# The FFN's last 64 inner rows: two tiles at a time on the two halves of the array's rows, each tile in a PSUM bank of its own

## The chip, the core and the metric

The kernel runs on one core of one Trainium2 chip, in one launch. A core has five engines with an instruction stream each: TensorE (PE; its weight loads are shown apart as PEld), VectorE (DVE), ScalarE (ACT), GpSimd (POOL) and SyncE (SP), which issues most of the DMA transfers. They meet at semaphores. Matmuls write to PSUM, which has 8 banks of 512 f32 in each of 128 partitions. The metric is the device time of one execution in microseconds (us).

## The reference, cut to what matters

Two layers work on x, 4 x 256 rows of 256 numbers (1,024 tokens, 8 tiles of 128 rows): a graph attention and an FFN, then a sparse graph step and a mixture of experts with two experts chosen per token. The change concerns the FFN of the first layer:

```python
g = jnp.einsum('th,ih->ti', xf, gate_w) * gate_s      # gate_w: 704 x 256
u = jnp.einsum('th,ih->ti', xf, up_w) * up_s          # up_w:   704 x 256
hdn = jax.nn.silu(g) * u
out = jnp.einsum('ti,hi->th', hdn, down_w) * down_s   # down_w: 256 x 704
```

Its result is added to x by way of a gate. The inner size 704 is five times 128 and 64 more. All of it is in f32.

## The kernel before, in words

The FFN works on two halves `h` of four tiles each. `ffn_up(h, it)` makes chunk `it` of the inner rows for the half's 512 tokens: PE multiplies the gate's weights (`gw`) and the up weights (`uw`) with the turned input `xnT`, ACT takes the silu into `th`, and DVE multiplies that with the up product into `hT` (L1475). Chunk 5 holds the last 64 inner rows: the 64 gate columns and the 64 up columns stand side by side in `gw`, so one product has the gate in rows 0 to 63 and the up product in rows 64 to 127; ACT writes rows 64 to 127 of `th`, DVE rows 64 to 127 of `hT`, and rows 0 to 63 of `hT` and of the down weights `dw` are zero.

`ffn_down(p, i)` (L2027) sums the six chunks for tile `i` of pair `p` in half a bank (banks 4 and 5), and DVE adds a pair's result to x (L1484). Every f32 matmul stands in the trace as two records, each with a weight load of its own; so a tile of `ffn_down` has twelve records and the FFN's two products with chunk 5 are two times four.

Nothing is scheduled automatically. `PE_ORDER`, `ACT_ORDER`, `DVE_ORDER` and `POOL_ORDER` are lists written by hand, and each engine walks through its list in order. So what stands behind a waiting step waits too. Around the change these steps stand in the lists:

- `lost` (L2039), `keep` (L1223, L1229) and `kept` (L2052): the sparse graph's exact threshold. DVE searches in small pieces (`search`, L1147 to L1177), PE counts the rows that the search has lost, DVE reads that flag and makes `a2`, PE turns `a2` in banks 6 and 7.
- `router` (L2072), `choices` to `ranks`, `count` (L2085), `list` (L2104) and `ids` (L1698, L1699): the experts' scores, and from them the list of the tokens of each expert. With `ids(0)` POOL gathers the tokens' rows (L699), and PE turns them in `turn_x` (L2114).
- `up1`, `up3` (both L2128) and `down` (L2160): the experts. `down(0)` waits until DVE has made the third pair's x (`attn_out`, L1513).
- SP loads `dw` and the scales `dsr` in `load_down` (L550 to L553), and DVE multiplies them in `scale_down` (L1271, L1272).

Of the kernel before, what the change touches and what calls it, by code (L numbers as in the profile page):

```python
# [63 lines left out]
def build(nc, x_in, ctx2_in, g_xattn, g_ffn, gamma, w0_in, w0T_in, b0_in, w1_in, w1T_in, a_in, b1_in,  # L64
# [5 lines left out]
    with ctx:  # L70
# [2262 lines left out]
```

## Time and profile before

| | us |
|---|---|
| median of 2 runs | 215.81 (215.25 to 216.37) |
| the profiled execution, as a run | 216.97 |
| its span in the trace | 215.1 |

The span is read from the first to the last instruction; the execution's own time has 1.9 us around it. Records of PE are pipelined: the ends are modelled, and how fast a stream goes is read from start to start. A group of records in the timeline has the start of the first, the time to the end of the last, and behind "x" how many there are. The granted clock is at its full level from 0 to 203 us of the span, and at 0.72 of it on the mean over the last 12 us.

### The profile page before, as it was taken

The numbers are of one execution on the slowest core, as the hardware profiler recorded it, in microseconds if no ns is written. First come the engines' busy times: TensorE is split into PE (matmuls) and PEld (weight loads), VectorE is DVE, ScalarE is ACT, GpSimd is POOL, SyncE is SP. The second block draws the span as 40 slices with busy tenths as digits, with TensorE's granted clock in tenths as the row PEclk, the third lists the DMA queues.
The fourth block names the chain that finished last, engine by engine and source line by source line (L and its number), as shares of the span: only waits on it lengthen the run. The fifth ranks groups of instructions, "written<-read, shape, count | busy, mean of one in ns | idle before, by whom it ended". The sixth has DMA issues, their size and how long they took to land.

```text
span 215.1 us, 3843 instructions
## 1 busy us (share of the span) xinstructions
PE 201.7 (94%) x1286; PEld 159.0 (74%) x1286; DVE 136.5 (63%) x469; ACT 84.9 (39%) x187; POOL 84.7 (39%) x107
## 2 busy tenths in 40 slices
PE   8999979999999999989999999999999999999930
PEld 7787854435786447869899999999963599999920
DVE  3497897999997989997987796933318511211210
ACT  2678662998300457033434272222226322222100
POOL 8175326620001120045460334667768155434143
PEclk9999999999999999999999999999999999999985
DMA  6838409219999216817044222232423210122224
GB/s 183 214 157 254 130 26 274 59 38 382 411 420 417 91 49 213 318 38 247 30 123 145 29 24 24 47 46 49 80 57 42 55 10 4 13 24 24 25 23 45
DMA packets 16795, 26.06 MB, mean 121 GB/s; under 512 B 4105, under 2 KB 12421, under 8 KB 16774
## 3 DMA queue, kind: packets, MB, share of 16 engines
q1 hardware_dynamic: 11328, 20.14, 26.0%
q0 software_dynamic: 4064, 5.24, 13.9%
q10 hardware_dynamic: 1382, 0.41, 1.1%
q8 instruction: 11, 0.18, 0.4%
q14 instruction: 10, 0.08, 0.1%
HBM read 21.34 MB, written 5.51 MB: 125 GB/s over the span
## 4 chain that ended last, share of the span: by engine, by line
PE 48%; DVE 22%; DMA 13%; issue 7%; POOL 3%; ACT 2%; POOLq 2%; DVEq 1%; ACTq 0%
PE PS L2128 13%; PE PS L2160 8%; DMA out_dram<-a,ids_late 8%; PE PS L2013 4%; DMA out_dram<-zb,sidx 4%; PE PS L1831 4%; PE PS L2180 3%; PE PS L2027 3%; PE PS L1895 2%; PE PS L2193 2%; DVE hT L1475 2%; ACT a L854 2%; PE PS L2072 2%; DVE x L1335 2%; DVE a L1229 1%
## 5 line engine op out<-in xcount | busy, mean ns | idle before, releaser
L2128 PE MATMUL PS<-hT,e 128*128 128x128 f32 x512 | 61.7, 275 | 0.0
L2128 PEld LDWEIGHTS PS<-hT,e 128*128 128x128 f32 x512 | 60.0, 192 | 1.0 <-issue 0.4
L2013 PE MATMUL PS<-xnT,e 128*128 128x512 f32 x88 | 39.5, 597 | 1.2 <-ACT xnT L923 0.8
L2013 PEld LDWEIGHTS PS<-xnT,e 128*128 128x128 f32 x88 | 16.2, 190 | 21.2 <-issue 17.4
L1731 DVE TENSOR_TENSOR hT<-th,PS 128x512 f32<-128x512 f32 x15 | 10.3, 687 | 32.5 <-PE PS L2128 31.1
L2160 PE MATMUL PS<-e,hT 128*128 128x256 f32 x128 | 30.4, 381 | 0.2 <-DVE x L1513 0.2
L2160 PEld LDWEIGHTS PS<-e,hT 128*128 128x128 f32 x128 | 23.2, 190 | 2.9 <-issue 0.3
L656 POOL TENSOR_TENSOR rstd<-veps,nhalf 128x2 f32<-128x2 f32 x12 | 8.7, 727 | 39.3 <-DVE veps L1092 39.2
L722 POOL DMA_INDIRECT out_dram<-a,ids_early x8 | 13.2, 1646 | 22.4 <-ACT a L1017 8.5
L2027 PE MATMUL PS<-e,hT 128*128 128x256 f32 x96 | 21.9, 383 | 0.0
L993 ACT ACTIVATE th<-PS 128x512 f32<-128x512 f32 x16 | 9.5, 593 | 26.7 <-PE PS L2128 26.7
L2027 PEld LDWEIGHTS PS<-e,hT 128*128 128x128 f32 x96 | 17.8, 190 | 2.8 <-issue 0.5
L722 POOL DMA_INDIRECT out_dram<-a,ids_late x7 | 11.1, 1581 | 15.1 <-DMA out_dram<-a,ids_late 10.8
L699 POOL DMA_INDIRECT sim<-xn_rows,ids_early x8 | 8.4, 1055 | 19.0 <-DVE ids_early L1699 13.8
L678 POOL DMA_INDIRECT e<-graph_rows,gix x8 | 9.2, 1156 | 9.7 <-DMA graph_rows<-e 8.0
L951 ACT ACTIVATE x<-x,rs 128x256 f32<-128x256 f32 x8 | 4.4, 594 | 19.4 <-DVEq L1507 19.4
L1831 PE MATMUL PS<-ones 128*128 128x128 f32 x64 | 10.8, 326 | 1.0 <-POOL ones L608 1.0
L1831 PEld LDWEIGHTS PS<-ones 128*128 128x128 f32 x64 | 9.5, 230 | 1.6 <-POOL ones L608 1.0
L1017 ACT ACTIVATE a<-PS,coef_early 128x256 f32<-128x256 f32 x8 | 3.8, 473 | 15.8 <-PE PS L2160 15.8
L854 ACT ACTIVATE a<-sim,bar 128x256 f32<-128x256 f32 x16 | 7.9, 497 | 3.8 <-DVE bar L1122 3.8
L699 POOL DMA_INDIRECT sim<-xn_rows,ids_late x8 | 8.4, 1046 | 2.4 <-issue 2.1
L1475 DVE SCALAR_TENSOR_TENSOR hT<-th,us,PS 128x512 f32<-128x512 f32 (+1 forms) x12 | 8.9, 746 | 0.2
(314 smaller groups left out, 321.3 us busy)
## 6 DMA issues: line engine op xcount, KB each, us to landing
e<-e_in SPq DMA_DIRECT2D x24, 512.0 KB, 8.3
x<-x_in SPq DMA_DIRECT2D x2, 512.0 KB, 5.9
graph_rows<-e SPq DMA_DIRECT2D x4, 256.0 KB, 2.2
out_dram<-x SPq DMA_DIRECT2D x4, 256.0 KB, 2.7
xn_rows<-xn SPq DMA_DIRECT2D x4, 256.0 KB, 2.6
e<-gw_in SPq DMA_DIRECT2D x1, 768.0 KB
e<-uw_in SPq DMA_DIRECT2D x1, 640.0 KB
e<-dw_in SPq DMA_DIRECT2D x1, 640.0 KB, 4.4
```

The lines of the kernel that those rows point to most:

```text
L678: pool.indirect_dma_start(out=picked[:, t, :], out_offset=None, in_=f_dram[b], in_offset=bass.IndirectOffsetOnAxis(ap=gix[:, t:t + 1], axi ...
L699: pool.indirect_dma_start(out=xg[j % E], out_offset=None, in_=xn3_dram[0:(HN, B * N)[h], :], in_offset=bass.IndirectOffsetOnAxis(ap=ids[h] ...
L722: pool.indirect_dma_start(out=out, out_offset=bass.IndirectOffsetOnAxis(ap=row_of, axis=0), in_=yv[kept_in(j)], in_offset=None, bounds_che ...
L854: ins = act.activation(a2[:, t, :], sim[:, t, :], ACT.Sign, bias=bar[:, n, t:t + 1], accum_out=signs[:, t:t + 1])
L993: act.activation(th[:, j % 2, :], PS[:, j % 2, :], ACT.Silu).then_inc(silu_ready, 1)
L1475: dve.scalar_tensor_tensor(out=hT[at:P, it, :], in0=th[at:P, n % 2, :], scalar=us[at:P, it:it + 1], in1=PS[at:P, bank, :], op0=ALU.mult, o ...
L1731: dve.tensor_tensor(hh[me], th[:, me, :], PS[:, 2 + me, :], ALU.mult).then_inc(gated, 1)
L1831: pe.matmul(PS[:, bank, 0:P], ones[:, :], ones[:, :], start=True, stop=True)
L2013: mm = pe.matmul(PS[:, bank, :], w[:, k, it * P:(it + 1) * P], xnT[:, h, k, :], start=(k == 0), stop=(k == 1))
L2027: mm = pe.matmul(PS[:, 4 + a // 2, (a % 2) * 256:(a % 2 + 1) * 256], hT[:, it, a * P:(a + 1) * P], dw[:, it, :], start=(it == 0), stop=(it ...
L2128: mm = pe.matmul(PS[:, bank + q, f * P:(f + 1) * P], w[:, k * F + f * P:k * F + (f + 1) * P], xgT[x_at][:, k, :], start=(k == 0), stop=(k ...
L2160: mm = pe.matmul(PS[:, y_bank(j), q * C:(q + 1) * C], hh[q][:, f * P:(f + 1) * P], W2[expert_of(j)][:, f * C:(f + 1) * C], start=(f == 0), ...
```

## The change

The 64 last inner rows of a tile now lie on either half of the partitions: for tiles 0 and 2 of a half of the tokens on rows 64 to 127, for tiles 1 and 3 on rows 0 to 63. `dw` holds the last 64 rows twice, `gw` has 64 columns more (up, gate, up), and the two zero fills on POOL are gone. In `ffn_up(h, 5)` PE multiplies tiles 0 and 2 with one choice of columns and tiles 1 and 3 with another (four matmuls of 2 x 128 columns in place of two of 512), and ACT and DVE do their step in two instructions of 64 x 256 in place of one of 64 x 512. A new step `ffn_tails(p)` multiplies the 64 rows of a pair's two tiles, one on each half of the rows, ahead of the pair's `ffn_down`, which has five chunks left. Each tile sums in a bank of its own (4 to 7 in place of halves of 4 and 5). `lost` moves from bank 6 to bank 3, so `ffn_up(1, 1)` waits until the flag has been read; `kept` waits until the half's sums have been read out of banks 6 and 7.

```diff
+GATE = FULL * P + 3 * TAIL
...
-        gw = e1[:, 5 * 1024:5 * 1024 + 2 * IT * P].rearrange("p (k n) -> p k n", k=2)
+        gw = e1[:, 5 * 1024:5 * 1024 + 2 * GATE].rearrange("p (k n) -> p k n", k=2)
...
+        DOWN_BANK = 4
+        LOST_BANK = 3
...
-                    ("router", 0), ("router", 1), ("ffn_down", 2, 0), ("count", 0), ("ffn_down", 2, 1), ("ffn_down", 3, 0, 0, 3),
-                    ("list", 0), ("ffn_down", 3, 0, 3), ("ffn_down", 3, 1, 0, 4), ("turn_x", 0), ("ffn_down", 3, 1, 4), ("lost", 1),
+                    ("router", 0), ("router", 1), ("ffn_tails", 2), ("ffn_down", 2, 0), ("count", 0), ("ffn_down", 2, 1), ("ffn_tails", 3), ("ffn_down", 3, 0, 0, 4),
+                    ("list", 0), ("ffn_down", 3, 0, 4), ("ffn_down", 3, 1, 0, 4), ("turn_x", 0), ("ffn_down", 3, 1, 4), ("lost", 1),
...
+        LOW, HIGH = slice(0, TAIL), slice(P - TAIL, P)
+        TAIL_ROWS = ((HIGH, LOW), (LOW, HIGH))
+
+        def every_second(ap, i):
+
+            return ap.rearrange("p (a i n) -> p a i n", i=2, n=P)[:, :, i, :]
...
-                sp.dma_start(dw[P - TAIL:P, FULL, :], dw_in[FULL * P:INTER, :]).then_inc(down_loaded, 16)
+                for r in (0, P - TAIL):
+                    sp.dma_start(dw[r:r + TAIL, FULL, :], dw_in[FULL * P:INTER, :]).then_inc(down_loaded, 16)
...
-            pool.memset(dw[0:P - TAIL, FULL, :], 0.0).then_inc(consts, 1)
-            pool.memset(hT[0:P - TAIL, FULL, :], 0.0).then_inc(consts, 1)
...
-                M, to = (P, 0) if it < FULL else (TAIL, P - TAIL)
-                act.activation(th[to:to + M, n % 2, :], PS[0:M, n % 2, :], ACT.Silu,
-                               scale=gs[0:M, it:it + 1]).then_inc(ffn_silu, 1)
+                if it < FULL:
+                    ins = act.activation(th[:, n % 2, :], PS[:, n % 2, :], ACT.Silu, scale=gs[:, it:it + 1])
+                else:
+                    for i, (rows_of_h, rows_of_gate) in enumerate(TAIL_ROWS):
+                        ins = act.activation(every_second(th[rows_of_h, n % 2, :], i), every_second(PS[rows_of_gate, n % 2, :], i),
+                                             ACT.Silu, scale=gs[rows_of_gate, it:it + 1])
+                ins.then_inc(ffn_silu, 1)
...
+                    for i, (rows_of_h, _) in enumerate(TAIL_ROWS):
+                        ins = dve.scalar_tensor_tensor(out=every_second(hT[rows_of_h, it, :], i), in0=every_second(th[rows_of_h, n % 2, :], i),
+                                                       scalar=us[rows_of_h, it:it + 1], in1=every_second(PS[rows_of_h, n % 2, :], i),
+                                                       op0=ALU.mult, op1=ALU.mult)
+                ins.then_inc(ffn_h_ready, 1)
...
-                dve.tensor_tensor(xp, xp, PS[:, bank, :].rearrange("p (t c) -> p t c", t=2),
-                                  ALU.add).then_inc(down_read, 1)
+                dve.tensor_tensor(xp, xp, PS[:, bank:bank + n, 0:C], ALU.add).then_inc(down_read, 1)
...
+                if it == FULL:
+                    for i, first in enumerate((FULL * P + TAIL, FULL * P)):
+                        for k in range(2):
+                            mm = pe.matmul(every_second(PS[:, n % 2, :], i), gw[:, k, first:first + P], every_second(xnT[:, h, k, :], i),
+                                           start=(k == 0), stop=(k == 1))
+                    mm.then_inc(ffn_g_done, 1)
+                    return
+                if h == 1 and 2 + n % 2 == LOST_BANK:
+                    pe.wait_ge(lost_ready, 1)
...
-            def ffn_down(p, i, first=0, stop=IT):
+            def ffn_tails(p):
+
+                first = PARTS[p][0] % HT
+                pe.wait_ge(ffn_h_ready, IT * (p // 2 + 1))
...
+                for i, (rows_of_h, _) in enumerate(TAIL_ROWS):
+                    a = first + i
+                    pe.matmul(PS[:, DOWN_BANK + a, 0:C], hT[rows_of_h, FULL, a * P:(a + 1) * P],
+                              dw[rows_of_h, FULL, :], start=True, stop=False)
+
+            def ffn_down(p, i, first=0, stop=FULL):
+
+                a = PARTS[p][0] % HT + i
                 for it in range(first, stop):
-                    mm = pe.matmul(PS[:, 4 + a // 2, (a % 2) * 256:(a % 2 + 1) * 256],
-                                   hT[:, it, a * P:(a + 1) * P], dw[:, it, :],
-                                   start=(it == 0), stop=(it == IT - 1))
+                    mm = pe.matmul(PS[:, DOWN_BANK + a, 0:C], hT[:, it, a * P:(a + 1) * P], dw[:, it, :],
+                                   start=False, stop=(it == FULL - 1))
...
                 pe.wait_ge(a2_ready, HT * (h + 1))
+                pe.wait_ge(down_read, 2 * (h + 1))
```

Two places in the built programs are needed below. In these rows "e" is the memory of the experts' weights, in which `gw`, `uw` and `dw` lie before the experts come; the lists count matmuls, of which each has two records in the trace.

PE in the second half of the FFN, from the last chunk's product to the step behind `turn_x(0)`. Before:

```order
L2013 MATMUL PS<-xnT,e 128x512 x2
L2072 MATMUL PS<-rg,xnT 128x8 x8
L2027 MATMUL PS<-e,hT 128x256 x6
L2085 MATMUL PS<-Os,before 128x40
L2085 MATMUL PS<-Os,ones 128x40 x4
L2027 MATMUL PS<-e,hT 128x256 x9
L2104 MATMUL PS<-RA,h0T 128x16 x8
L2027 MATMUL PS<-e,hT 128x256 x7
L2114 MATMUL PS<-ident,sim 128x128 x2
L2027 MATMUL PS<-e,hT 128x256 x2
```

In the change (L2031 is the last chunk of `ffn_up`, L2056 `ffn_tails`, L2063 `ffn_down`, L2140 `list`, L2150 `turn_x`):

```order
L2031 MATMUL PS<-xnT,e 128x2x128 x4
L2108 MATMUL PS<-rg,xnT 128x8 x8
L2056 MATMUL PS<-e,hT 128x256 x2
L2063 MATMUL PS<-e,hT 128x256 x5
L2121 MATMUL PS<-Os,before 128x40
L2121 MATMUL PS<-Os,ones 128x40 x4
L2063 MATMUL PS<-e,hT 128x256 x5
L2056 MATMUL PS<-e,hT 128x256 x2
L2063 MATMUL PS<-e,hT 128x256 x4
L2140 MATMUL PS<-RA,h0T 128x16 x8
L2063 MATMUL PS<-e,hT 128x256 x5
L2150 MATMUL PS<-ident,sim 128x128 x2
```

Ahead of `list(0)` stood 6 + 9 = 15 full matmuls; now there are 5 + 5 + 4 = 14 full ones and two pairs on halves. Behind it, up to `turn_x(0)`, stand 5 in place of 7.

DVE at the last chunk of the second half (the DVE list keeps its order). Before:

```order
L1166 MAX top<-work 128x8 x2
L1475 SCALAR_TENSOR_TENSOR hT<-th,us,PS 64x512
L1533 COPY sc<-PS 128x16
L1537 MAX mx<-sc 128x8 x2
L1540 MAX_INDEX ix<-mx,sc 128x8 x2
```

In the change:

```order
L1179 MAX top<-work 128x8 x2
L1492 SCALAR_TENSOR_TENSOR hT<-th,us,PS 64x2x128 x2
L1550 COPY sc<-PS 128x16
L1554 MAX mx<-sc 128x8 x2
L1557 MAX_INDEX ix<-mx,sc 128x8 x2
```

One instruction has become two of half the width, ahead of the reading of the scores; ACT has the same in its `ffn_up` of the last chunk.

## Rows read from the trace of the kernel before

**Rows 1.** The page's first part: busy us, share of the span, instructions.

```profile
PE 201.7 (94%) x1286; PEld 159.0 (74%) x1286; DVE 136.5 (63%) x469; ACT 84.9 (39%) x187; POOL 84.7 (39%) x107
```

**Rows 2.** The chain of waits in order of time, 72 to 110 us: start, us, what.

```profile
73.13 0.76 DVE hT L1475
73.94 7.13 PE PS L2013 x16
...
85.44 2.73 PE PS L2027 x12
...
88.30 3.97 PE PS L2027 x18
92.27 0.20 PE PS L2104 x8
92.49 0.18 DVE rest_early L1698
...
107.14 1.97 PE PS L2160 x8
```

**Rows 3.** PE's timeline at two earlier steps on half rows (64*64, 64*128): start, us.

```profile
19.65 0.38 PE L1895 MATMUL PS<-w1x,h0T 128*128 128x256 f32 x1
19.96 1.07 PE L1847 MATMUL PS<-ctx,wbuf 64*64 64x512 f32 x4
20.97 0.39 PE L1980 MATMUL PS<-norms,ones 128*128 128x5 f32 x2
...
23.16 0.38 PE L1895 MATMUL PS<-w1x,h0T 128*128 128x256 f32 x1
23.47 2.00 PE L1856 MATMUL PS<-ctx,th 64*128 64x256 f32 x16
25.40 0.29 PE L1903 MATMUL PS<-ident,e 128*128 128x128 bf16 x2
```

**Rows 4.** PE's timeline, 40 to 112 us.

```profile
50.26 5.32 PE L2013 MATMUL PS<-xnT,e 128*128 128x512 f32 x12
55.41 7.93 PE L2027 MATMUL PS<-e,hT 128*128 128x256 f32 x36
63.18 0.17 PE L2039 MATMUL PS<-lost,ones 128*128 128x1 bf16 x1
...
69.32 1.04 PE L2052 MATMUL PS<-ident,a 128*128 128x128 f32 x8
```

**Rows 5.** ACT's timeline: four instructions of 256 columns in a row; the last silu.

```profile
7.20 1.57 ACT L883 ACTIVATE zb<-PS,b 128x256 f32<-128x256 f32 x4 [3.69 <-PE PS L1882]
...
83.79 0.68 ACT L944 ACTIVATE th<-PS,gs 64x512 f32<-64x512 f32 x1 [0.94 <-PE PS L2013]
```

**Rows 6.** DVE's timeline, 38 to 85 us.

```profile
38.66 0.35 DVE L1271 TENSOR_SCALAR dsr<-dsr,tg 128x256 f32<-128x256 f32 x1
...
45.71 0.88 DVE L1335 SCALAR_TENSOR_TENSOR x<-e,tg,x 128x256 f32<-128x256 f32 x2
...
52.99 0.75 DVE L1475 SCALAR_TENSOR_TENSOR hT<-th,us,PS 64x512 f32<-64x512 f32 x1
...
68.38 0.68 DVE L1484 TENSOR_TENSOR x<-x,PS 128x512 f32<-128x512 f32 x1
...
71.88 1.22 DVE L1495 TENSOR_TENSOR zb<-a,PS 128x1024 f32<-128x1024 f32 x1
...
84.50 0.75 DVE L1475 SCALAR_TENSOR_TENSOR hT<-th,us,PS 64x512 f32<-64x512 f32 x1
```

**Rows 7.** Who waited for whom: us in total, times, longest us.

```profile
PE PS L2114 <- DMA sim<-xn_rows,ids_early: 1.0, 1, 1.0
...
DVE rest_early L1698 <- PE PS L2104: 0.2, 1, 0.2
```

**Rows 8.** SP's timeline: the issue of the load of the down scales.

```profile
33.64 0.58 SPq L553 DMA_DIRECT2D dsr<-ds_in  x1
```

**Rows 9.** DMA issues: KB each, median us from issue to landing.

```profile
dsr<-ds_in SPq DMA_DIRECT2D x1, 128.0 KB, 4.5
```

More of the change, by code:

```diff
@@ L428, in build @@
                     ("ffn_up", 0, 4), ("turn_ffn", 2), ("turn_ffn", 3), ("ffn_up", 0, 5), ("ffn_up", 1, 0),
-                    ("ffn_down", 0, 0), ("ffn_down", 0, 1), ("ffn_down", 1, 0), ("lost", 0), ("ffn_down", 1, 1), ("ffn_up", 1, 1),
+                    ("ffn_tails", 0), ("ffn_down", 0, 0), ("ffn_down", 0, 1), ("ffn_tails", 1), ("ffn_down", 1, 0), ("lost", 0), ("ffn_down", 1, 1), ("ffn_up", 1, 1),
                     ("kept", 0), ("ffn_up", 1, 2), ("ffn_up", 1, 3), ("ffn_up", 1, 4), ("turn_moe", 0), ("turn_moe", 1), ("ffn_up", 1, 5),
-                    ("router", 0), ("router", 1), ("ffn_down", 2, 0), ("count", 0), ("ffn_down", 2, 1), ("ffn_down", 3, 0, 0, 3),
-                    ("list", 0), ("ffn_down", 3, 0, 3), ("ffn_down", 3, 1, 0, 4), ("turn_x", 0), ("ffn_down", 3, 1, 4), ("lost", 1),
+                    ("router", 0), ("router", 1), ("ffn_tails", 2), ("ffn_down", 2, 0), ("count", 0), ("ffn_down", 2, 1), ("ffn_tails", 3), ("ffn_down", 3, 0, 0, 4),
+                    ("list", 0), ("ffn_down", 3, 0, 4), ("ffn_down", 3, 1, 0, 4), ("turn_x", 0), ("ffn_down", 3, 1, 4), ("lost", 1),
                     ("up1", 0), ("turn_x", 1), ("up3", 0),
@@ L1222, in keep @@
                 dve.wait_ge(lost_counted, h + 1)
-                dve.tensor_scalar(flag[:, 1 + h:2 + h], PS[:, 6, 0:1], 1.0, None, ALU.min).then_inc(lost_ready, 1)
+                dve.tensor_scalar(flag[:, 1 + h:2 + h], PS[:, LOST_BANK, 0:1], 1.0, None, ALU.min).then_inc(lost_ready, 1)
                 dve.wait_ge(lost_ready, h + 1)
@@ L2010, in ffn_up @@
                     pe.wait_ge(xnT_copied, XT["turn_ffn", 2 * h + 1] + 1)
-                for w, bank, ready in ((gw, n % 2, ffn_g_done), (uw, 2 + n % 2, ffn_u_done))[0:2 if it < FULL else 1]:
+                if it == FULL:
[7 more added lines that the diff above has]
+                    pe.wait_ge(lost_ready, 1)
+                for w, bank, ready in ((gw, n % 2, ffn_g_done), (uw, 2 + n % 2, ffn_u_done)):
                     for k in range(2):
@@ L2038, in lost @@
                 pe.wait_ge(found_ready, h + 1)
-                pe.matmul(PS[:, 6, 0:1], ones16[:, :], lost16[:, h:h + 1], start=True, stop=True)\
+                pe.matmul(PS[:, LOST_BANK, 0:1], ones16[:, :], lost16[:, h:h + 1], start=True, stop=True)\
                   .then_inc(lost_counted, 1)
@@ L2199, in _ @@
                          hot=graph_hot, choice=choice, compose=compose, stay_warm=stay_warm,
-                         flag=graph_flag, graph_check=graph_check, turn_ffn=turn_ffn, ffn_up=ffn_up, ffn_down=ffn_down, lost=lost, kept=kept,
+                         flag=graph_flag, graph_check=graph_check, turn_ffn=turn_ffn, ffn_up=ffn_up, ffn_tails=ffn_tails, ffn_down=ffn_down, lost=lost, kept=kept,
                          turn_moe=turn_moe, router=router)
@@ L2287, with columns @@
     full = FULL * P
-    def columns(v, at):
-        last = np.zeros(P, v.dtype)
-        last[at:at + TAIL] = v[full:]
-        return np.concatenate([v[:full], last]).reshape(IT, P).T
+    def columns(v):
+        return np.concatenate([v, v[full:]]).reshape(IT, P).T
     def by_head(layer):
@@ L2317 @@
         "a_in": np.stack([by_head("0"), by_head("1")]), "b1_in": i["L0_xattn_b1"],
-        "gw_in": np.concatenate([i["L0_ffn_gate_w"], i["L0_ffn_up_w"][full:]]).T,
+        "gw_in": np.concatenate([i["L0_ffn_gate_w"][:full], i["L0_ffn_up_w"][full:], i["L0_ffn_gate_w"][full:],
+                                 i["L0_ffn_up_w"][full:]]).T,
         "uw_in": i["L0_ffn_up_w"][:full].T, "dw_in": i["L0_ffn_down_w"].T,
-        "gs_in": columns(i["L0_ffn_gate_s"], 0), "us_in": columns(i["L0_ffn_up_s"], P - TAIL), "ds_in": i["L0_ffn_down_s"],
+        "gs_in": columns(i["L0_ffn_gate_s"]), "us_in": columns(i["L0_ffn_up_s"]), "ds_in": i["L0_ffn_down_s"],
         "wq_in": np.concatenate([i["L1_xattn_Wq"]] * 2, axis=1), "wk_in": i["L1_xattn_Wk"], "rg_in": i["L1_ffn_gate_w"].T,
```

24 lines of the change are left out of this document (12 added, 12 removed).

## The prediction

> **What bounds the kernel now.** The page's first part shows PE busy for 94% of the span and DVE for 63% [rows 1]. That average invites a wrong conclusion, that less work on PE is less time; so I read the chain of waits next, in order of time, around the FFN's sums. From 73.94 to 92.27 us the chain lies on PE without a break: chunks 3 and 4 of the second half, the last chunk, the router, twelve records of `ffn_down`, eighteen more, and the eight of `list(0)`. Then it leaves PE: DVE makes the list's ids at 92.49 and stays on the chain until PE's `down(0)` at 107.14 [rows 2]. The view of who waited for whom has DVE waiting 0.2 us for `list(0)`, and PE waiting 1.0 us for the first gathered rows behind it [rows 7]. So ahead of `list(0)` PE is the bound, and how early `list(0)` stands is what counts; behind it PE has time to spare, and from 107.14 on it is the bound again, with an order that the change leaves alone. What the FFN's first half gains on PE meets a DVE that is behind: `kept(0)` starts at 69.32, `attn(0)` takes its result only at 71.88 [rows 4, 6], and PE's products of 73.94 follow DVE's product of 73.13 [rows 2].
>
> One slot, below, is a full f32 record of 256 columns from start to start: 36 records of `ffn_down` from 55.41 to 63.18, 0.216 us each [rows 4]; one of 512 columns is 5.15 / 12 = 0.43 us.
>
> **What a pair on half rows costs.** The kernel has such steps already [rows 3]. Sixteen half records of 256 columns begin at 23.47 and the next step at 25.40: 1.93 us, where sixteen slots would be 3.45. So two halves do run at once: eight slots are 1.73. But the step pays something beside its slots. From the last full record ahead (23.16) to the first one behind (25.40) it is 2.24 us, and nine slots are 1.94: 0.30 over. The other step is just like one `ffn_tails`, two matmuls on two halves, of 512 columns: from 19.65 to 20.97 it is 1.32 us, and 0.216 + 2 x 0.43 = 1.08: 0.24 over. I take 0.27 for a step that goes from full rows to halves and back. Then the first full record behind it: in the sums of `ffn_down` that begin behind other work, twelve records take 2.73 us in place of 2.59 and eighteen take 3.97 in place of 3.89 [rows 2], 0.08 to 0.14 over; I take 0.11. Together 0.38 for each `ffn_tails`, and what it saves is two slots, 0.43. **One pair at a time gains 0.05 us on PE**, not 0.43, and four of them 0.2 us in the whole kernel, not 1.73.
>
> The Trainium skill, TensorEngine Tiling (Array Packing), section Key Properties, states that a change of the tiling mode drains TensorE; the 0.24 and 0.30 agree with it. The same page's section Theoretical Speedup gives up to 2 times for a small dimension of at most 64, and by that alone four pairs would save 1.73.
>
> **Part by part, on the chain.**
>
> 1. The list stands later. Between the router and `list(0)` stood 12 + 18 = 30 full records. The first two sums have lost a chunk each (four slots less) and `ffn_tails` comes twice (four more), but of pair 3's first tile four chunks stand ahead of the list in place of three: 32 slots. **+0.43 us**, even with switches at no cost.
> 2. The two switches in that stretch. The one of pair 3 lies in the middle of full records: 0.38. That of pair 2 follows the router, whose first full record already pays 0.11, and 0.07 of the way in hides under the wait of part 4: 0.20. **+0.58**; the ends are 0 (all hidden) and 0.9 (0.44 twice).
> 3. The last chunk of the first half. ACT has two silus of 256 columns in place of one of 512: four such instructions in a row take 1.57 [rows 5], so two 0.79, in place of 0.68. DVE has two products in place of one: two of 256 columns take 0.88, one 0.75 [rows 6]. The chain lies on DVE there, and this product at 52.99 is in it, up to PE's 73.94. 0.13 + 0.11, less a few hundredths that ACT is ahead: **+0.2**; ends 0 and 0.3.
> 4. The same in the second half: the silu at 83.79 ends at 84.47 and DVE starts at 84.50 and ends at 85.25, PE's sums follow within 0.2 us. The sums start 0.24 later, less what PE has in hand: **+0.2**; ends 0 and 0.4.
> 5. The product of the last chunk on PE itself: eight records of 256 columns in place of four of 512: 8 x 0.216 = 1.73 and 4 x 0.43 = 1.72. **0**, if the gap between the two runs of 128 columns costs nothing (a rival).
> 6. New waits. `kept(0)` now waits for DVE's second sum, which ends at 68.38 + 0.68 = 69.06, with part 3 at 69.26; it started at 69.32. PE comes there no earlier than before by more than 0.1, and DVE wants its result at 71.88 [rows 4, 6]. `ffn_up(1, 1)` waits for the flag that DVE reads right behind `lost(0)` at 63.18, and PE still has five full matmuls to do. `ffn_tails(3)` waits for the router's scores, read ahead of `count(0)`. **0**; up to 0.3 if DVE is later than I think, and 2.5 us of cover stand behind it.
> 7. The loads. SP issues one transfer more ahead of `dsr`; such an issue takes 0.58, so `dsr`, issued at 33.64 and 4.5 us on its way, lands at 38.7 in place of 38.1 [rows 8, 9], and DVE wants it at 38.66 [rows 6]. **0**; at most 0.2, with 64 KB more in the way. `gw`, 64 KB larger, comes long ahead of the FFN. POOL's two fills stand at the start of the kernel, and no link of the chain comes from them: 0.
> 8. DVE's sums read two banks in place of one, the same 512 numbers: 0; ends -0.1 and +0.1.
>
> Sum: 0.43 + 0.58 + 0.2 + 0.2 = **1.4 us**. The shift passes on: DVE comes to `ids(0)` 1.4 later, works without a wait until `attn_out`, and `down(0)` moves with it. PE's 0.86 us fewer slots behind the list only lengthen its wait for the gathered rows, from 1.0 to about 2. The profiled execution took 216.97 us, so 218.4 for one like it; the median of the two runs is 1.16 lower, 215.81, and from it I forecast **217.2 us**. The ends of the parts give +0.4 to +2.2, so 216.2 to 218.0.
>
> **The rivals.**
>
> - *The switches are hidden* at these places, as weights come ahead of the full matmuls elsewhere. Parts 1, 3 and 4 stay: +0.8, 216.6. Against it: both steps in rows 3 pay. Chance 0.17.
> - *The halves do not overlap here*, say because two matmuls alone give no overlap. Four slots a step in place of two: 2 x 0.43 more on the chain, +2.3, 218.1. Against it: the step of two matmuls at 19.96 did overlap. Chance 0.08.
> - *Not slower: PE's own time decides.* If DVE's chain has slack that the view does not show, the four pairs give 0.2 to 1.7 us: 214.1 to 215.6, say 215.1. For it: 94% busy. Against it: the chain leaves PE twice just where the change acts. Chance 0.13.
> - *Slower by over 2%: the gap costs.* The last chunk's products now read and write two runs of 128 columns with as much between them; no row of before has a matmul of f32 that does so. If such a record took two slots, the eight in each half cost 1.73 more; both halves' lie on the chain (ACT waited 0.94 for PE ahead of the silu at 83.79 [rows 5]): +1.4 + 3.5, 220.7. It decides from 0.18 us more for a record, since 2% are 4.3 us. Chance 0.06. The Trainium skill, PSUM — Partial Sum Buffer, section Specifications (TRN2), states that any non-contiguous access pattern slows matmuls significantly; no run here shows it.
>
> The forecast itself has 0.56.
>
> **The numbers.** Predicted 217.2; for the forecast alone 216.2 to 218.0. The range of 215.3 to 218.7 takes in the hidden switches, halves that don't overlap and half of the not-slower case, with the 0.5 us by which the two runs lie from their median. A measurement of this kernel tells about 2% from no change, 4.3 us; the whole last chunk of the sums is 16 x 0.216 = 3.45 us, so faster by 2% is nearly excluded: 0.02. Slower by 2% has the gap's case and little else: 0.05. Within 2%: 0.93.
>
> **What would show it.** In the profile after: `list(0)` should stand about 1.4 us later than 92.1, with DVE waiting over 1 us for it in place of 0.2; PE's wait for the first gathered rows about 2 us; each `ffn_tails` with four records in two starts, and from the last full record ahead of it to the first behind 0.9 us or more, not 0.65; ACT's and DVE's last chunk 0.1 longer each; and `down(0)` near 108.5. I am wrong if `list(0)` comes at 92.5 or earlier, if `down(0)` moves less than DVE's ids, or if the eight records of the last chunk take over 1.8 us.

## The result, and the profile after

The changed kernel took **219.33 us** (median of 2 runs, 218.97 and 219.70), the kernel before 215.81: ratio 1.0159, 95% interval 1.0103 to 1.0215. Six later runs gave 218.86 (`control` below). The forecast was 217.2, its range ended at 218.7. The profiled execution took 219.70, its span 217.7 (before 216.97 and 215.1).

The page's first part, after; it answers to [rows 1].

```profile
PE 203.3 (93%) x1294; PEld 159.7 (73%) x1294; DVE 136.9 (63%) x471; ACT 85.8 (39%) x189; POOL 84.9 (39%) x105
```

The chain of waits, after (start, us, what), which answers to [rows 2].

```profile
73.74 0.76 DVE hT L1488
74.54 7.13 PE PS L2039 x16
...
92.48 1.92 PE PS L2063 x8
...
95.83 2.91 DMA sim<-xn_rows,ids_early
98.88 0.54 PE PS L2150 x2
```

Before, DVE stayed on the chain from the ids at 92.49 to `down(0)`. Now the chain goes from the gather to PE's `turn_x(0)` (L2150) and stays on PE up to `kept(1)`, ahead of DVE's last steps to `down(0)`: PE itself is late behind its wait.

PE's timeline, after (L2031 last chunk, L2108 router, L2056 `ffn_tails`, L2063 sums, L2121 `count(0)`, L2140 `list(0)`, L2164 `up1(0)`, L2196 `down(0)`).

```profile
82.48 1.89 PE L2031 MATMUL PS<-xnT,e 128*128 128x256 f32 x8
84.21 1.85 PE L2108 MATMUL PS<-rg,xnT 128*128 128x8 f32 x16
86.42 0.70 PE L2056 MATMUL PS<-e,hT 64*128 64x256 f32 x4 [0.36 <-DVE hT L1492]
87.05 2.42 PE L2063 MATMUL PS<-e,hT 128*128 128x256 f32 x10
89.31 0.19 PE L2121 MATMUL PS<-Os,before 128*128 128x40 bf16 x1
...
89.44 2.40 PE L2063 MATMUL PS<-e,hT 128*128 128x256 f32 x10
91.78 0.70 PE L2056 MATMUL PS<-e,hT 64*128 64x256 f32 x4
92.41 1.99 PE L2063 MATMUL PS<-e,hT 128*128 128x256 f32 x8
94.24 0.35 PE L2140 MATMUL PS<-RA,h0T 128*128 128x16 bf16 x8
...
98.88 0.54 PE L2150 MATMUL PS<-ident,sim 128*128 128x128 f32 x2 [2.03 <-DMA sim<-xn_rows,ids_early]
...
100.14 3.12 PE L2164 MATMUL PS<-hT,e 128*128 128x128 f32 x16
...
110.12 1.97 PE L2196 MATMUL PS<-e,hT 128*128 128x256 f32 x8 [0.19 <-DVE x L1530]
```

The same places before (L2027 sums, L2104 `list(0)`, L2114 `turn_x(0)`, L2128 `up1(0)`, L2160 `down(0)`).

```profile
85.31 2.86 PE L2027 MATMUL PS<-e,hT 128*128 128x256 f32 x12
...
88.14 4.13 PE L2027 MATMUL PS<-e,hT 128*128 128x256 f32 x18
92.11 0.35 PE L2104 MATMUL PS<-RA,h0T 128*128 128x16 bf16 x8
...
96.61 0.41 PE L2114 MATMUL PS<-ident,sim 128*128 128x128 f32 x2 [1.03 <-DMA sim<-xn_rows,ids_early]
...
97.75 2.03 PE L2128 MATMUL PS<-hT,e 128*128 128x128 f32 x16
...
107.14 1.97 PE L2160 MATMUL PS<-e,hT 128*128 128x256 f32 x8 [0.19 <-DVE x L1513]
```

`list(0)` stands 2.13 later than before, `down(0)` 2.98. And `up1(0)` takes 3.12 us where it took 2.03. The view by stretches of time says why. It gives each engine's busy time, and its last three columns are the granted clock (1.00 is 2.4 GHz), the DMA share and GB/s.

```profile
98.90:99.40 0.50, 0.50 (x3) 0.50 (x4) 0.43 (x3) 0.00 (x0) 0.50 (x1) 0.62 0.81 246
99.40:102.00 2.60, 2.60 (x13) 2.19 (x12) 2.46 (x10) 0.38 (x1) 1.86 (x3) 0.50 0.51 106
102.00:103.20 1.20, 1.20 (x10) 1.20 (x10) 0.95 (x8) 0.00 (x0) 0.51 (x1) 0.82 0.90 317
```

Right behind PE's 2.03 us without work the granted clock lay at its lower level, 1.2 GHz: by these three means for 0.38 + 2.60 + 0.43 = 3.4 us. Before, behind 1.03 us [rows 7], it stayed at 2.4 GHz. No part of the prediction had this.

DVE and ACT, after, at the places of [rows 5, 6].

```profile
39.14 0.57 DVE L1284 TENSOR_SCALAR dsr<-dsr,tg 128x256 f32<-128x256 f32 x1 [0.36 <-issue]
...
53.60 0.49 DVE L1492 SCALAR_TENSOR_TENSOR hT<-th,us,PS 64x256 f32<-64x256 f32 x1 [0.22 <-ACT th L956]
...
85.39 0.97 DVE L1492 SCALAR_TENSOR_TENSOR hT<-th,us,PS 64x256 f32<-64x256 f32 x2 [0.34 <-ACT th L956]
...
94.63 0.17 DVE L1715 TENSOR_SCALAR rest_early<-PS 128x8 f32<-128x8 f32 x1 [1.32 <-PE PS L2140]
```

```profile
84.41 0.95 ACT L956 ACTIVATE th<-PS,gs 64x256 f32<-64x256 f32 x2 [0.95 <-PE PS L2031]
```

DVE waits where it did not, or hardly did: ahead of its scaling of `dsr` (the view names no releaser there), for the second silu in both halves, and for `list(0)` (0.2 before).

**One clock for all profiles.** DVE's first FFN product comes up to 1 us earlier in one execution than in another. Counted from that product (37.68 before, 37.71 after), the profiles agree to some hundredths where nothing was changed. All places below are counted so. The first sum is the first record of PE's `ffn_tails` or `ffn_down` behind the router.

| from DVE's first FFN product, us | before | after | control | load_early | all_piped |
|---|---|---|---|---|---|
| (that product itself, from the span's start) | 37.68 | 37.71 | 37.72 | 36.82 | 37.26 |
| first sum of the second half | 47.63 | 48.71 | 48.32 | 48.30 | 47.65 |
| `count(0)` | 50.33 | 51.60 | 51.22 | 51.20 | 51.19 |
| `list(0)` | 54.43 | 56.53 | 56.14 | 56.13 | 53.96 |
| `turn_x(0)` | 58.93 | 61.17 | 60.72 | 60.71 | 58.79 |
| `down(0)` | 69.46 | 72.41 | 72.07 | 71.29 | 69.42 |

So the 2.95 us at `down(0)` are 1.08 up to the first sum, 0.19 from there to `count(0)`, 0.83 from `count(0)` to `list(0)`, 0.14 in the gather and 0.71 behind it. The experiments look for the cause of each; the 0.14 got none. (In `all_piped`, below, the first sum is of a chunk that does not wait for the last one, and `count(0)` stands three chunks later in PE's list.)

### The profile page after: what moved, and what is told of

Same layout as the page of the kernel before. It is cut to its first block, busy times and chain, and to the rows that moved or that the text cites. A ratio compares the mean times of both kernels' runs of the same rounds, so it can differ in the third digit from the quotient of the medians.

```text
span 217.7 us, 3860 instructions
## 1 busy us (share of the span) xinstructions
PE 203.3 (93%) x1294; PEld 159.7 (73%) x1294; DVE 136.9 (63%) x471; ACT 85.8 (39%) x189; POOL 84.9 (39%) x105
## 4 chain that ended last, share of the span: by engine, by line
PE 53%; DVE 16%; DMA 15%; issue 8%; POOL 2%; ACT 2%; POOLq 2%; DVEq 1%; ACTq 0%
PE PS L2164 16%; PE PS L2196 8%; DMA out_dram<-a,ids_late 7%; DMA out_dram<-zb,sidx 6%; PE PS L2039 5%; PE PS L1848 3%; PE PS L2063 3%; PE PS L2216 3%; PE PS L2229 2%; DVE hT L1488 2%; PE PS L2150 2%; PE PS L2031 2%; PE PS L1912 2%; PE PS L1899 1%; DMA sim<-xn_rows,ids_early 1%
## 5 line engine op out<-in xcount | busy, mean ns | idle before, releaser
L2164 PE MATMUL PS<-hT,e 128*128 128x128 f32 x512 | 62.8, 278 | 0.0
L2164 PEld LDWEIGHTS PS<-hT,e 128*128 128x128 f32 x512 | 61.1, 195 | 1.1 <-issue 0.6
L2039 PE MATMUL PS<-xnT,e 128*128 128x512 f32 x80 | 36.1, 599 | 1.4 <-ACT xnT L932 0.8
L2196 PE MATMUL PS<-e,hT 128*128 128x256 f32 x128 | 30.4, 381 | 0.2 <-DVE x L1530 0.2
L2039 PEld LDWEIGHTS PS<-xnT,e 128*128 128x128 f32 x80 | 14.7, 190 | 20.4 <-issue 15.8
L2196 PEld LDWEIGHTS PS<-e,hT 128*128 128x128 f32 x128 | 23.2, 190 | 2.9 <-issue 0.3
L2063 PE MATMUL PS<-e,hT 128*128 128x256 f32 x80 | 19.5, 394 | 0.0
L2063 PEld LDWEIGHTS PS<-e,hT 128*128 128x128 f32 x80 | 14.8, 193 | 3.1 <-issue 1.3
L687 POOL DMA_INDIRECT e<-graph_rows,gix x8 | 9.9, 1236 | 9.7 <-DMA graph_rows<-e 8.0
L996 ACT ACTIVATE hT<-PS 128x256 f32<-128x256 f32 x16 | 6.1, 378 | 7.9 <-PE PS L2150 7.9
```

Of the source, the lines that this page charges most:

```text
L687: pool.indirect_dma_start(out=picked[:, t, :], out_offset=None, in_=f_dram[b], in_offset=bass.IndirectOffsetOnAxis(ap=gix[:, t:t + 1], axi ...
L2039: mm = pe.matmul(PS[:, bank, :], w[:, k, it * P:(it + 1) * P], xnT[:, h, k, :], start=(k == 0), stop=(k == 1))
L2063: mm = pe.matmul(PS[:, DOWN_BANK + a, 0:C], hT[:, it, a * P:(a + 1) * P], dw[:, it, :], start=False, stop=(it == FULL - 1))
L2164: mm = pe.matmul(PS[:, bank + q, f * P:(f + 1) * P], w[:, k * F + f * P:k * F + (f + 1) * P], xgT[x_at][:, k, :], start=(k == 0), stop=(k ...
L2196: mm = pe.matmul(PS[:, y_bank(j), q * C:(q + 1) * C], hh[q][:, f * P:(f + 1) * P], W2[expert_of(j)][:, f * C:(f + 1) * C], start=(f == 0), ...
```

## The experiments

Fourteen kernels, in four groups that each shared their runs of the kernel before (medians 216.23, 216.02, 215.73, 216.10).

**control**: the changed kernel again.

> The changed kernel once more, beside the others on one chip, for the spread of its executions. Theory: one fall of the granted clock behind turn_x(0) in most executions, a second one at 86 us in some, and so executions from 217.6 (none) by 218.9 (one) to 220.2 (two), median 219.0. Rival (the one profile of the changed kernel was an exception): a single group near 218.0.

Measured: 218.86 (218.39 to 219.64), ratio 1.0156 [1.0109, 1.0203]. The mean granted clock of the six runs is 0.973 once (219.64), 0.979 to 0.981 three times (218.78 to 219.61) and 0.988 to 0.989 twice (218.39, 218.53). The lower clock does go with the longer time, but the steps are about half of what was expected, and at the highest clock it is 218.4 to 218.5, not 217.6. (Only one of the six has a trace; that these two had no fall is read from the mean clock.) In `load_early`, below, which keeps the order of the changed kernel, the six runs are 217.6 and 217.7 at 0.986 to 0.988, 218.4 and 219.3 at 0.979, 219.8 and 220.2 at 0.971 to 0.973: there the steps are near 1.2. So what a fall costs in a run's time stays open between some 0.5 and 1.2 us. Either way more than half of the loss is there without one: 1.6 of 2.85 us in `load_early`, 2.7 of 3.1 here.

**list_early**: `list(0)` six full records earlier.

```diff
-("ffn_tails", 3), ("ffn_down", 3, 0, 0, 4), ("list", 0), ("ffn_down", 3, 0, 4)
+("ffn_tails", 3), ("ffn_down", 3, 0, 0, 1), ("list", 0), ("ffn_down", 3, 0, 1)
```

> The changed kernel with list(0) behind the first chunk of pair 3's first tile, not behind the fourth: six full records, 1.30 us, earlier. Theory (the loss is that list(0) comes late, PE then stands idle for 2.03 us at turn_x(0), and the granted clock falls to half right behind that): list(0) at about 92.9 in place of 94.24, DVE's ids wait under 0.1 in place of 1.32, PE's idle time ahead of turn_x(0) about 0.75, no fall of the clock at 99 us and up1(0) in 2.03 in place of 3.12; down(0) near 108.1 in place of 110.12, the time 2.0 us under the changed kernel's. Rival 1 (the fall of the clock comes from something else in the change, not from the idle time): the fall stays, gain 1.3. Rival 2 (PE's own work decides): no gain, 0 within 0.3.

Measured: 217.72, ratio 1.0058 [1.0033, 1.0082]. PE's timeline:

```profile
85.64 0.70 PE L2056 MATMUL PS<-e,hT 64*128 64x256 f32 x4 [0.36 <-DVE hT L1492]
86.28 3.79 PE L2063 MATMUL PS<-e,hT 128*128 128x256 f32 x10
...
98.40 0.41 PE L2150 MATMUL PS<-ident,sim 128*128 128x128 f32 x2 [0.68 <-DMA sim<-xn_rows,ids_early]
...
99.47 2.02 PE L2164 MATMUL PS<-hT,e 128*128 128x128 f32 x16
```

The wait at `turn_x(0)` shrank to 0.68 and the fall behind it is gone, as expected: from `turn_x(0)` to `down(0)` it is 10.58 us, as before (10.53). The gain was 1.1 us against `control` and 1.6 against the first two runs; set against the kernel before of its own group it is 2.1 (1.0156 less 1.0058), so the 2.0 is not excluded. What was not expected: in this profile the clock fell at another place, at 87 us, where ten records of sums take 3.79 in place of 2.42. Ahead of that PE had the router's sixteen short records and 0.36 us of waiting. Of its nine runs, three have a mean clock of 0.976 to 0.977 (218.1 to 218.9), one 0.983 (218.2), five 0.990 to 0.992 (216.5 to 217.7).

**warm**: unread matmuls in PE's wait.

```diff
-("ffn_down", 3, 1, 0, 4), ("turn_x", 0)
+("ffn_down", 3, 1, 0, 4), ("stay_warm", 7, 1), ("turn_x", 0)
```

> The changed kernel with seven matmuls of 128 columns that nobody reads, in bank 1, between the last sum ahead of turn_x(0) and turn_x(0): PE works on for about 1.7 of the 2.03 us in which it waited for the gathered rows. Nothing else moves: list(0) at 94.24 and turn_x(0) at 98.88 as in the changed kernel. Theory (the idle time let the clock fall): the granted clock stays full from 98 to 103 us, up1(0) takes 2.03 in place of 3.12, down(0) near 109.4 in place of 110.12, the time 0.7 us under the changed kernel's. Rival 1 (the fall has nothing to do with the idle time): clock as in the changed kernel, 0. Rival 2 (DVE decides down(0) anyway): the clock stays full, but down(0) stays near 110.1, 0.

Measured: 217.81, ratio 1.0074 [1.0050, 1.0098].

```profile
97.27 1.72 PE L1848 MATMUL PS<-ones 128*128 128x128 f32 x14
99.49 0.41 PE L2150 MATMUL PS<-ident,sim 128*128 128x128 f32 x2 [0.50 <-DMA sim<-xn_rows,ids_early]
...
100.46 2.02 PE L2164 MATMUL PS<-hT,e 128*128 128x128 f32 x16
```

With 1.72 us more work on PE the kernel is faster by 1.0 us against `control`, by the two ratios 1.8: no fall behind `turn_x(0)`, and 10.51 us from there to `down(0)` in place of 11.35 in `control`. (In this profile the clock fell at 86 us, where ten records of sums take 3.96 us, so its `list(0)` is later than expected.)

**before_list_late**: the kernel before, `list(0)` six records later and nothing else.

```diff
-("ffn_down", 3, 0, 0, 3), ("list", 0), ("ffn_down", 3, 0, 3)
+("ffn_down", 3, 0), ("list", 0)
```

> The kernel before, with list(0) behind all six chunks of pair 3's first tile, not behind three: six full records, 1.30 us, later. No half-row step, no doubled rows, no split instruction: only the place of list(0). Theory: list(0) at 93.4, DVE waits 1.45 for it, PE's idle time ahead of turn_x(0) 2.3 in place of 1.03, and the granted clock falls to half behind it for some us as in the changed kernel; down(0) 1.3 + 0.7 = 2.0 later, near 109.1. Rival 1 (the fall of the clock needs something of the change): no fall, down(0) 1.3 later. Rival 2 (DVE has slack between ids and down(0)): under 0.5 later.

Measured: 218.12, ratio 1.0080 [1.0053, 1.0107].

```profile
97.32 0.41 PE L2114 MATMUL PS<-ident,sim 128*128 128x128 f32 x2 [2.37 <-DMA sim<-xn_rows,ids_early]
...
99.28 2.87 PE L2128 MATMUL PS<-hT,e 128*128 128x128 f32 x16
```

`list(0)` came 1.31 later and `down(0)` 2.57, with `turn_x(0)` to `down(0)` 11.74. The fall needs nothing of the change but the late list. Over the sixteen profiles of this document: PE waited 1.96 to 2.37 us at `turn_x(0)` in seven, and in five of them the clock fell behind it (11.2 to 11.7 us from there to `down(0)`); it waited 0.50 to 1.71 in nine, and behind that it fell in none (10.4 to 10.6). In `load_early` (1.98) and `one_tails` (2.06) it did not fall: such a wait costs 0.7 to 1.2 us in some executions, not in all.

**dsr_first** and **load_early**: the loads.

```diff
 def load_down():                                # dsr_first
+    sp.dma_start(dsr[:, :], rows(ds_in)).then_inc(down_loaded, 16)
     sp.dma_start(dw[:, 0:FULL, :], ...)
...
     load_general()                              # load_early
+    sp.dma_start(dw[0:TAIL, FULL, :], dw_in[FULL * P:INTER, :]).then_inc(down_loaded, 16)
```

> The changed kernel with SP issuing the load of the down scales ahead of the down weights, not behind them and their doubled last 64 rows. Theory (the one issue more makes DVE's scale_down 0.4 late, and DVE never makes that up before list(0)): DVE's scaling of dsr starts at 38.66 in place of 39.14, ffn_up(0, 1) on DVE at 40.7 in place of 41.42, list(0) 0.43 earlier, the time 0.4 to 0.5 us under the changed kernel's. Rival (there is slack on DVE between 41 and 52 us, or the last 64 rows themselves land as late): list(0) as in the changed kernel, 0.

> The changed kernel with the added copy of the down weights' last 64 rows issued by SP ahead of the up weights' users, some 15 us earlier, so that SP's issues at 32 to 35 us are those of the kernel before. The load of dsr first did not help, since DVE then waited 1.19 us for the last 64 rows, which came last. Theory (one transfer more ahead of DVE's scale_down costs 0.2 to 0.6 us, and DVE never makes that up): DVE's idle time ahead of its scaling of dsr is 0 as before, scaling in 0.35, the time 0.3 to 0.5 us under the changed kernel's. Rival (the transfers land late for another reason, or the slack hides it): the wait stays 0.2 or more, no gain.

Measured: `dsr_first` 219.68, ratio 1.0164 [1.0121, 1.0206]; `load_early` 218.87, ratio 1.0138 [1.0103, 1.0173]. DVE's scaling of `dsr`, first in `dsr_first`, then in `load_early`:

```profile
39.21 0.35 DVE L1284 TENSOR_SCALAR dsr<-dsr,tg 128x256 f32<-128x256 f32 x1 [1.19 <-DMA e<-dw_in]
```

```profile
37.81 0.35 DVE L1284 TENSOR_SCALAR dsr<-dsr,tg 128x256 f32<-128x256 f32 x1
```

`dsr_first` failed by its rival: what comes last is waited for, whichever it is. `load_early`, where the added copy no longer stands ahead of `dsr`, takes the wait away. In `list_early`, which has the loads of the changed kernel, the view names the load as the releaser:

```profile
38.46 0.47 DVE L1284 TENSOR_SCALAR dsr<-dsr,tg 128x256 f32<-128x256 f32 x1 [0.46 <-DMA dsr<-ds_in]
```

What the wait costs depends on when the load lands. In all eight profiles with these loads DVE comes to `dsr` 4.4 us behind SP's issue of it, while before it came 5.0 behind (33.64 and 38.66). In four of them it starts at once, in the other four 4.6 to 4.9 us behind the issue. `control` has no wait and is 0.39 ahead of `after` at the first sum, 0.34 at `down(0)`; `warm`, with 0.18 us of waiting, is not late at the first sum (48.31), `list_early` with 0.46 is (48.71). The times of `load_early` and `control` overlap, so this is read from profiles, not from medians.

**before_split**: the kernel before, ACT's and DVE's last chunk in two instructions each.

```diff
-act.activation(th[to:to + M, n % 2, :], PS[0:M, n % 2, :], ...)
+for cols in (slice(0, 256), slice(256, 512)):   # the last chunk; DVE's product likewise
+    ins = act.activation(th[to:to + M, n % 2, cols], PS[0:M, n % 2, cols], ...)
```

> The kernel before, with the last chunk's silu on ACT and its product on DVE each in two instructions of 256 columns in place of one of 512, in both halves of the tokens; PE's products, its sums and the order stay. Theory (parts 3 and 4 of the prediction, by the trace after 0.2 and 0.38): DVE's product of the second half ends 0.3 to 0.4 later, list(0) 0.3 to 0.6 later and the time 0.4 to 0.6 over the kernel before's. Rival (the two instructions hide beside other work): 0 within 0.2.

Measured: 216.80, ratio 1.0035 [1.0012, 1.0059].

```profile
84.55 0.89 DVE L1478 SCALAR_TENSOR_TENSOR hT<-th,us,PS 64x256 f32<-64x256 f32 x2 [0.20 <-ACT th L945]
```

The first sum stands at 48.11, 0.48 later, and `down(0)` at 69.94, 0.48 later too. ACT's two silus take 0.82 us here (at 83.69), DVE's two products 0.89. In the changed kernel it is 0.69 at the first sum (`control`), with 0.95 and 0.97. Its instructions read every second block of 128 columns and lie on two halves of the rows; which of the two makes them longer is not shown.

**piped**: the two tile groups of the last chunk in banks of their own, so that DVE can start behind the first silu.

```diff
-every_second(PS[:, n % 2, :], i)                 # PE, ACT, DVE
+every_second(PS[:, n % 2 + 2 * i, :], i)
+    if i == 0: ins.then_inc(ffn_silu, 1)         # ACT, behind the first silu
+    dve.wait_ge(ffn_silu, n + 1 + h + i)         # DVE, ahead of each product
```

> The changed kernel with that edit alone: two banks for the last chunk, and DVE's first product behind the first silu. Theory: ffn_tails(2) and list(0) 0.5 earlier against DVE's first FFN product (list(0) 55.6 us behind it in place of 56.14), the time 0.5 under the changed kernel's, with falls of the clock as there, since the idle time at turn_x(0) stays. Rival (two instructions are longer work in themselves): list(0) at 56.0 or later.

Measured: 218.35, ratio 1.0101 [1.0074, 1.0128]. Its DVE row for the second half, which answers to the one of the changed kernel above with 0.34 us of waiting:

```profile
83.73 0.98 DVE L1495 SCALAR_TENSOR_TENSOR hT<-th,us,PS 64x256 f32<-64x256 f32 x2
```

No wait is left, the instructions are as long as before (0.96 and 0.98 us), and `list(0)` is at 55.66 where 55.6 was expected. So of the 0.69, 0.48 goes when DVE need not wait for the second silu, and 0.2 stays.

**one_tails**: the second half's four tails in one step.

```diff
-("ffn_tails", 2), ("ffn_down", 2, 0), ("count", 0), ("ffn_down", 2, 1), ("ffn_tails", 3)
+("ffn_down", 2, 0), ("count", 0), ("ffn_down", 2, 1), ("ffn_tails", 2)   # all four tiles
```

> The changed kernel with the second half's four tails in one step behind the sums of pair 2, not in two steps of two; list(0) stays behind the fourth chunk of pair 3's first tile, and the sums of pair 2 still wait for the whole last chunk. The half-row matmuls are as many, but PE switches to halves and back once in place of twice. Theory (a switch costs about 0.38 us and lies on PE's way to list(0)): from the first record of pair 2's sums to list(0) 7.4 us in place of 94.24 - 86.42 = 7.82; list(0) 0.4 earlier, and with it the time by 0.4 where the clock behaves as in the changed kernel. Rival (the switch is hidden, the loss lies in the slots alone): 7.8, no gain.

Measured: 218.91, ratio 1.0139 [1.0115, 1.0162]. PE, and DVE's input for `count(0)`:

```profile
85.25 2.42 PE L2067 MATMUL PS<-e,hT 128*128 128x256 f32 x10 [0.37 <-DVE hT L1492]
87.77 0.20 PE L2125 MATMUL PS<-Os,before 128*128 128x40 bf16 x1
...
90.24 1.13 PE L2055 MATMUL PS<-e,hT 64*128 64x256 f32 x8
91.30 1.99 PE L2067 MATMUL PS<-e,hT 128*128 128x256 f32 x8
93.14 0.35 PE L2144 MATMUL PS<-RA,h0T 128*128 128x16 bf16 x8
```

```profile
87.41 0.30 DVE L1568 TENSOR_TENSOR Os<-O 128x32 bf16<-128x32 f32 x1
```

From the first sum to `list(0)` 7.89, not 7.4: no gain. The step itself is cheap: eight records in 1.06 us, where two steps of four take 0.63 each. But part of the saved time went into a new wait: `count(0)` at 87.77 comes right behind DVE's `Os` (87.71), about 0.25 later than ten slots of 0.216 and the first record's 0.1 allow.

**sums_first**: pair 2's full chunks straight behind the router, `count(0)` three chunks later, all tails in one step, and `list(0)` one chunk behind it.

```diff
-("router", 1), ("ffn_tails", 2), ("ffn_down", 2, 0), ("count", 0), ("ffn_down", 2, 1), ("ffn_tails", 3),
-("ffn_down", 3, 0, 0, 4), ("list", 0), ("ffn_down", 3, 0, 4)
+("router", 1), ("ffn_down", 2, 0), ("ffn_down", 2, 1, 0, 3), ("count", 0), ("ffn_down", 2, 1, 3),
+("ffn_tails", 2), ("ffn_down", 3, 0, 0, 1), ("list", 0), ("ffn_down", 3, 0, 1)
```

> The changed kernel with the second half's sums in another order: pair 2's full chunks directly behind the router, which do not wait for the last chunk, count(0) three chunks later, then all four tails in one step, one chunk of pair 3, list(0). Theory (the granted clock falls where PE has had too little to do, and that is at two places: the router's 16 short records and the wait of 0.36 us behind them, after which it fell to half at 87 us in the profiles of list_early, warm and dsr_first, and the idle time at turn_x(0)): with the first place filled and list(0) as early as DVE allows, about 92.7, there is no fall at either place; up1(0) in 2.0, down(0) near 107.9, the time about 1.2 us under that of list_early, 216.5, and its executions lie within 0.8 us of each other in place of the two groups, 216.5 to 217.0 and 217.7 to 218.9, that list_early shows. Rival (the fall at 87 us comes from elsewhere, and the two groups remain): 217.3 or more, with two groups.

Measured: 216.91, ratio 1.0035 [1.0016, 1.0053], ten runs from 216.05 to 217.59. No run has a mean clock under 0.986, and the profile has no fall. But the spread is 1.5, not 0.8, and the median 0.4 over what was expected: the clock is not all that differs between executions. `list(0)` comes earlier than before (54.11) and PE waits 0.24 for DVE within it; `down(0)` is at 69.88, 0.42 late.

**list_early_warm**: `list_early` with unread matmuls in the other wait.

```diff
-("router", 1), ("ffn_tails", 2)
+("router", 1), ("stay_warm", 2, 3), ("ffn_tails", 2)
```

> The kernel list_early (the changed kernel with list(0) three chunks earlier) with two matmuls of 128 columns that nobody reads, in bank 3, between the router and ffn_tails(2): PE works on for 0.43 us where it waited 0.36 us for DVE's last product. Theory (the executions of list_early at 217.7 to 218.9 are those in which the clock fell to half at 87 us, behind the router's short records and that wait): fewer or none of them, a mean granted clock of 0.985 or more in nearly every execution, the median at 216.5 to 217.1. Rival (that wait has nothing to do with the fall): two groups as in list_early, median 217.7.

Measured: 216.87; eleven of twelve runs have a mean clock of 0.987 or more, one 0.980 (219.72). That speaks for the wait as cause, but the ratio, 1.0058 [1.0026, 1.0090], is that of `list_early`: on the time this is inconclusive.

**before_five**: no last chunk in the sums.

```diff
-for it in range(first, stop):
+for it in range(first, min(stop, FULL)):
```

> The kernel before without the FFN's last chunk in the sums: PE leaves out the 16 matmuls of 256 columns with the last 64 inner rows (their part of the output is missing), everything else is as before. That is 32 records or 6.9 us of PE's stream in the whole, 16 records or 3.45 us in each half of the tokens, twice what the change could take from PE with halves at no cost. Theory (PE's time ahead of list(0) is worth only the 0.17 us that DVE waits there, and PE's time behind it only lengthens its idle time): list(0) 0.2 to 0.3 earlier, PE idle for some 2.5 us at turn_x(0) in place of 1.03, the granted clock falls to half behind that, and the time is 215.7 to 217.0 with the kernel before at 216.0. Rival (PE at 94% is the bound): 209 to 213.

The counts in that text are twice too high: 8 matmuls or 16 records are left out, 1.73 us of PE in each half, 3.45 in all. Measured: 233.98, which answers nothing, since with other sums the experts get other tokens and the program runs another way behind them (its step `up_over`, L2180, has 64 records in place of 32). Up to `down(0)` it can be read:

```profile
91.78 0.35 PE L2104 MATMUL PS<-RA,h0T 128*128 128x16 bf16 x8
...
107.01 1.97 PE L2160 MATMUL PS<-e,hT 128*128 128x256 f32 x8 [0.19 <-issue]
```

From DVE's first product (37.81) `list(0)` is at 53.97, 0.46 earlier, and `down(0)` at 69.20, **0.26 earlier for 3.45 us of PE's work**. That is the most that any saving on the tails could give here.

**all_three** (`sums_first` and `load_early` together) and **all_piped** (that and `piped`).

> The kernel sums_first with the added copy of the last 64 rows loaded early, as in load_early: the best that these experiments point to. Theory: no fall of the clock, no wait for dsr; what is left over the kernel before is the split of the last chunk on ACT and DVE, 0.4 to 0.8 us in before_split and here; 216.4 to 216.8, not under the kernel before. Rival 1 (the saved PE time is worth something once nothing else is late): under 215.8. Rival 2 (the load costs nothing in most executions): as sums_first, 216.9.

> The kernel all_three with the last chunk's two tile groups in banks of their own (1 and 3), and DVE's first product of the last chunk behind the first silu, not behind both. Theory (what is left of the loss is DVE's wait for the second silu, 0.22 us in the first half and 0.33 in the second): no idle time of DVE ahead of either, down(0) 0.5 earlier against DVE's first FFN product (69.4 us behind it in place of 69.9; 69.5 in the kernel before), the time 0.5 under all_three and within 0.4 of the kernel before. Rival (the two instructions are longer work in themselves): 0.1 or less, as all_three. Under the kernel before by more than 0.5 would mean that PE's saved time is worth something after all.

Measured: `all_three` 216.42, ratio 1.0027 [0.9998, 1.0056]; `all_piped` **216.04**, ratio **0.9989 [0.9965, 1.0013]**. `down(0)` stands at 69.91 and 69.42, where 69.4 was expected of the latter and the kernel before has 69.46. With every late step mended the time cannot be told from that of the kernel before.

## Why the prediction was wrong

The direction was right: slower, by a late `list(0)`, and within 2% on the median. The sum was 1.4 and the profile shows 2.95 at `down(0)`.

| term | predicted | measured | shown by |
|---|---|---|---|
| 1, 2 `list(0)` two slots later, switch of pair 3 | 0.43 + 0.38 | 0.83 | `count(0)` to `list(0)` |
| 2 switch of pair 2 | 0.20 | 0.19 | first sum to `count(0)` |
| 3, 4 last chunk split on ACT and DVE | 0.4 | 0.69 | `control`; `piped` gives 0.48 back |
| 5 strided product | 0 | 0 | L2031 x8, then 84.21 - 82.48 = 1.73 |
| 6 new waits | 0 | 0 | none of the three in the profile |
| 7 loads | 0 to 0.2 | 0.39 (0 in `control`) | `after`, `load_early` |
| the gather | not in it | 0.14 | `list(0)` to `turn_x(0)`; cause not shown |
| the clock behind PE's wait | not in it | 0.71 | `warm`, `list_early`, `before_list_late` |

- **Parts 1 and 2 hold.** From 89.44 to `list(0)` at 94.24 eighteen full records and a pair's step take 4.80 us, where eighteen alone took 3.97 (88.14 to 92.11): a step costs 0.83, the four full records that it replaces 0.86. It gains 0.03 us where 0.05 was worked out. The Trainium skill's drain at a change of the tiling mode (TensorEngine Tiling (Array Packing), Key Properties) agrees with that; as an estimate from the same page's Theoretical Speedup alone, the Trainium skill would give the step 0.43.
- **Parts 3 and 4 were mis-sized.** The mechanism held: the sums start later by what two silus and two products take longer than one. The sizes came from rows with contiguous columns, 0.79 and 0.88 us; here the pairs take 0.95 and 0.97. `before_split`, with contiguous columns, measured 0.82 and 0.89, and 0.48 at the first sum, near the 0.4 of the prediction. That DVE stands idle for 0.22 and 0.34 us until the second silu is the same loss seen from DVE; the prediction did not see that a count for each silu would save it (`piped`, 0.48).
- **Part 7 failed in the profiled execution.** It took an even race between the landing at 38.7 and DVE at 38.66 as no cost, with 4.5 us on the way as the one profile before had it. DVE comes 4.4 us behind the issue now, and the load takes up to 4.9, so it is late in some executions, and all of DVE's later work with it.
- **The step that failed outright** is the sentence that PE's fewer slots "only lengthen its wait for the gathered rows, from 1.0 to about 2". They did (2.03 us), and that wait was not free: the granted clock fell to 1.2 GHz for 3.4 us, and `down(0)` came 0.71 later by it. PE takes 8.01 us from `turn_x(0)` to `kept(1)` where it took 7.27, and is on the chain, where the prediction had it with time to spare. The profile before showed the clock full behind 1.03 us, and I read no further.
- **The rivals.** "PE's own time decides" is refuted by `before_five` and `warm`; "the halves do not overlap" by four records in 0.63 us, where four slots are 0.86; "the gap costs" by part 5: the Trainium skill's rule on non-contiguous patterns (PSUM — Partial Sum Buffer, Specifications (TRN2)) does not show at runs of 128 columns. "The switches are hidden" is refuted by the 0.83.
- **Two slips in the working.** The step at 19.96 is not "just like" an `ffn_tails`: it is of 64*64, two quarters of the array, and `ffn_tails` of 64*128. And the ends that the parts state add up to +0.3 to +2.6, not to +0.4 to +2.2; the measured time lies above both, so neither slip decided.

The medians lie 3.5 us apart (3.1 for `control`), the places of `down(0)` 2.95 (2.61). The 0.5 to 0.6 us between are not assigned. Behind `down(0)` the profiles (without `before_five`) take 106.6 to 108.0 us to the end of the span, whichever the kernel, and the start wanders by 1 us; two runs do not settle a difference below that. Open too is what makes such a wait lower the clock in one execution and not in the next.

## What to carry to other kernels

Where the chain leaves an engine, the engine's saved time only makes its wait longer, and a longer wait of PE can cost granted clock behind it: look at the row behind the wait, here `up1(0)`, not at the busy share. An instruction that is split in two should hand over each piece by itself, with a bank and a count of its own, or the pieces cost a serial step. A transfer that lands just in time in one profile can be late in the next execution.

## What the runs showed of the hardware

- The granted clock fell for some 3.4 us at a time, at two places of one kernel: behind PE's wait of 2.0 us, and behind sixteen records of 8 columns with 0.36 us of waiting (ten records of sums then took 3.79 us in place of 2.42). One profile, `dsr_first`, has both, and its run took 220.54.
- Four matmuls on halves in a row take 1.06 us to the next full record, two take 0.63: each further pair costs its two slots only.
- Counted from DVE's first FFN product, the first sum stands at 48.30 to 48.32 in `control`, `load_early`, `warm` and `one_tails`, while that product itself comes at 36.8 to 37.8 us in the sixteen profiles. A wait for one load moves it: 48.71 in `after` and `list_early`.
- The load of `dsr`, 128 KB, let DVE start as it came, 4.4 us behind the issue, in four profiles, and only 4.6 to 4.9 us behind it in four others of the same loads.
